# Counting the routed rows on VectorE instead of TensorE, in a two-layer attention and mixture-of-experts kernel

## The reference

```python
# layer 0, experts: 4096 rows, 8 choices (7 experts, 512 places each, and a no-op)
topk_vals, topk_idx = jax.lax.top_k(softmax(x @ router_w.T + router_b), 2)
expert_mask = (rows chosen by each expert)
sorted_indices = jnp.argsort(-expert_mask, axis=0)[:cap]      # the first 512 rows of each expert
h = relu(inputs @ experts_inter); out = (h @ experts_out) * weight     # added back at the rows' places
# layer 1, experts: 12 choices (8 experts and 4 that return the row), nothing is dropped
topk_logits, topk_idx = jax.lax.top_k(x @ gate_w.T + expert_bias, 2)
out = sum over the two of softmax weight * (expert's silu block, or x itself)
```

## Time and profile before

| | |
|---|---|
| median of 3 runs | 1630.83 us (1629.79 to 1632.42) |
| profiled execution | 1632.42 us, with a span of 1630.9 us |
| busy, PE / PEld / DVE / ACT / POOL | 85% / 59% / 54% / 43% / 30% |
| chain that ended last, by engine | PE 51%, DVE 5%, issue 5%, ACT 4%, DMA 3%, POOL 1% |
| TensorE's granted clock, mean | 0.925 of full speed |
| the five matmuls of `ps` | 16 times, once for each sequence in each layer |

### The profile page before, as it was taken

How to read it: one execution, slowest core, us unless ns; L and a number is a source line. 1 busy time by engine, 2 the same in 40 slices (tenths; PEclk the granted TensorE clock), 3 DMA queues, 4 the chain that set the end, 5 groups by cost and what they waited for, 6 DMA issues and landing times.

```text
span 1630.9 us, 31041 instructions
## 1 busy us (share of the span) xinstructions
PE 1383.5 (85%) x10703; PEld 959.3 (59%) x10704; DVE 879.5 (54%) x2705; ACT 702.2 (43%) x984; POOL 496.1 (30%) x415
## 2 busy tenths in 40 slices
PE   3779998999988289999449999999998659999991
PEld 1456666666655256767225555655655449999991
DVE  1667878778885311111357776776552443444344
ACT  2144555555556111110145767767777212222223
POOL 4032344334425311221111132233212134444442
PEclk7799999999999589999779999999999769999996
DMA  6845446536612035351165645644554434444446
GB/s 166 219 104 121 106 109 147 123 99 150 122 45 88 17 78 146 85 148 14 39 130 104 124 88 123 147 105 94 124 119 136 143 93 66 74 71 71 70 62 218
DMA packets 119545, 174.71 MB, mean 107 GB/s; under 512 B 17623, under 2 KB 101617, under 8 KB 113280
## 3 DMA queue, kind: packets, MB, share of 16 engines
q1 hardware_dynamic: 96320, 148.05, 37.5%
q0 software_dynamic: 20400, 22.37, 8.6%
q10 hardware_dynamic: 2704, 2.70, 0.5%
HBM read 107.64 MB, written 72.69 MB: 111 GB/s over the span
## 4 chain that ended last, share of the span: by engine, by line
PE 51%; DVE 5%; issue 5%; ACT 4%; DMA 3%; POOL 1%; SPq 1%; POOLq 0%; ACTq 0%; DVEq 0%
PE ST L1887 8%; PE shared L1899 7%; PE ST L1345 6%; PE ST L753 6%; PE OT L771 6%; PE shared L1547 3%; ACT arena L897 3%; PE OT L1355 3%; PE shared L1355 3%; PE shared L802 2%; PE shared L819 2%; PE shared L1554 1%; PE shared L783 1%; DMA arena<-qk_parts 1%; PE shared L1877 1%
## 5 line engine op out<-in xcount | busy, mean ns | idle before, releaser
L897 ACT ACTIVATE arena<-ST 128x1024 f32<-128x1024 f32 x416 | 411.6, 1024 | 207.2 <-PE ST L753 206.2
L753 PE MATMUL ST<-arena 96*128 96x256 bf16 (+2 forms) x1792 | 243.1, 270 | 36.6 <-DMA arena<-qk_parts 21.1
L771 PE MATMUL OT<-arena,v_aug 128*32 128x256 f32 (+1 forms) x3584 | 233.4, 375 | 8.2 <-POOL arena L1244 7.9
L753 PEld LDWEIGHTS ST<-arena 96*128 96x128 bf16 (+1 forms) x1792 | 149.9, 99 | 138.2 <-issue 47.8
L1994 POOL DMA_INDIRECT sum<-arena,block_to_row x71 | 112.2, 1581 | 167.9 <-DMA sum<-arena,block_to_row 115.1
L771 PEld LDWEIGHTS OT<-arena,v_aug 128*32 128x32 f32 x3584 | 91.4, 110 | 98.1 <-issue 47.9
L1899 PE MATMUL shared<-arena 128*128 x568 | 134.2, 379 | 0.0
L1244 POOL TENSOR_SCALAR_AFFINE_SELECT arena<-arena 128x512 f32<-128x512 f32 (+1 forms) x96 | 79.2, 831 | 170.3 <-ACT arena L897 170.3
L1716 POOL DMA_INDIRECT slot_x<-x_out,row_to x64 | 63.6, 994 | 163.5 <-DVE keep L1634 146.5
L1899 PEld LDWEIGHTS shared<-arena 128*128 128x128 f32 x568 | 102.6, 191 | 11.0
L1701 POOL TENSOR_TENSOR qk_src<-qk_rest,qk_src 128x512 bf16<-128x512 f32 x32 | 38.5, 1202 | 222.0 <-DVE qk_src L1671 222.0
(11 more groups left out here) (244 smaller groups left out, 2530.2 us busy)
## 6 DMA issues: line engine op xcount, KB each, us to landing
arena<-qk_parts SPq DMA_DIRECT2D x224, 128.0 KB, 6.9
qk_parts<-qk_src SPq DMA_DIRECT2D x32, 384.0 KB, 2.8
arena<-qk_parts SPq DMA_DIRECT2D x32, 384.0 KB, 4.6
qk_parts<-qk_src SPq DMA_DIRECT2D x64, 192.0 KB, 3.2
arena<-slot_x SPq DMA_DIRECT2D x71, 130.0 KB, 2.4
arena<-qk_parts SPq DMA_DIRECT2D x32, 256.0 KB, 5.4
sum<-x_out SPq DMA_DIRECT2D x16, 512.0 KB, 2.9
arena<-in_experts_inter SPq DMA_DIRECT2D x7, 1024.0 KB, 5.0
```

Of the source, the lines that this page charges most:

```text
L753: mm = pe.matmul(scores[:, i * 256 + at:i * 256 + at + nq], K[par][0:rows, h, kb * P:(kb + 1) * P], Q[par][0:rows, h, q0:q0 + nq], start=T ...
L771: mm = pe.matmul(OT[32 * i:32 * i + 32, q0:q0 + nq], v_aug[par][:, kb, g * GH + i, :], PT[n % RING][:, i, at:at + nq], start=(u == 0), sto ...
L897: act.activation(PT[n % RING][:, :, :], scores[:, :].rearrange("p (h n) -> p h n", h=GH), func, scale=ATT_SCALE).then_inc(L["exp"], 1)
```

## The change

The per-block sums move from TensorE to VectorE. A new tile `r_before` (128 by 5 by 12, bf16) replaces `r_carry` and `r_count`. Behind the mask, `count_before` copies block 4 of it to block 0 and then adds the mask block by block: five instructions, each waited for by the next, since each reads what the last one wrote. `ps` becomes eight matmuls of 8 or 12 columns, two for each block. It waits for the end of the five. The reduction and the carry's addition in `l3` go. In the schedule, `l2` has five more pieces in both layers, and stage A has four fewer spaces ahead of `ps`.

```diff
-N_ROUTE = {True: (3, 17, 11), False: (13, 0, 11)}
+N_ROUTE = {True: (3, 22, 11), False: (13, 5, 11)}
-SPACES = {True: (4, 2, 2, 0, 8), False: (4, 2, 4, 2, 4)}
+SPACES = {True: (4, 2, 2, 0, 4), False: (4, 2, 4, 2, 4)}
...
-                sums = bank[:, 0:TB * ne].rearrange("p (t e) -> p t e", t=TB)
-                pe.matmul(sums, before[:, :], r_mask[:, :, 0:ne], start=True, stop=False, skip_group_check=True)
-                for t in range(1, TB):
-                    pe.matmul(sums[:, t:TB, :], ones_b[:, :], r_mask[:, 0:TB - t, 0:ne], start=False, stop=False,
-                              skip_group_check=True)
-                pe.matmul(sums, ones_b[:, :], r_carry[k % 2][:, 0:ne].unsqueeze(1).broadcast_to([P, TB, ne]),
-                          start=False, stop=True, skip_group_check=True).then_inc(ready, 1)
+                for t in range(TB):
+                    pe.matmul(bank[:, t * ne:(t + 1) * ne], before[:, :], r_mask[:, t, 0:ne],
+                              start=True, stop=False)
+                    mm = pe.matmul(bank[:, t * ne:(t + 1) * ne], ones_b[:, :], r_before[:, t, 0:ne],
+                                   start=False, stop=True)
+                mm.then_inc(ready, 1)
...
-        def count_rows(dve, chain, ne):
-            chain.unwaited(dve.tensor_reduce(r_count[:, 0:ne], r_mask[:, :, 0:ne].rearrange("p t e -> p e t"),
-                                             AX_X, ALU.add))
-        def carry_on(dve, chain, ne, k):
-            chain.unwaited(dve.tensor_tensor(r_carry[(k + 1) % 2][:, 0:ne], r_carry[k % 2][:, 0:ne], r_count[:, 0:ne],
-                                             ALU.add))
+        def count_before(dve, chain, ne):
+            yield from chain(dve.tensor_copy(r_before[:, 0, 0:ne], r_before[:, TB, 0:ne]))
+            for t in range(TB):
+                yield from chain(dve.tensor_tensor(r_before[:, t + 1, 0:ne], r_before[:, t, 0:ne], r_mask[:, t, 0:ne],
+                                        ALU.add))
...
                 yield from chain(dve.tensor_tensor(r_mask[:, :, 0:ne], oh[0], oh[1], ALU.add))
+                yield from count_before(dve, chain, ne)
...
-                        act.wait_ge(L["rc"], k * ROUTE1 + MASK1 - 1)
+                        act.wait_ge(L["rc"], k * ROUTE1 + MASK1 - 5)
```

More of the change, by code:

```diff
@@ L542, in build @@
         r_mask = sb("r_mask", [P, TB, NEM], BF16)
-        r_carry = [sb(f"r_carry{i}", [P, NEM], BF16) for i in range(2)]
-        r_count = sb("r_count", [P, NEM])
+        r_before = sb("r_before", [P, TB + 1, NEM], BF16)
         row_to = [sb(f"row_to{i}", [P, TB, 2], I32) for i in range(2)]
@@ L595, in build @@
         TOLD, PLACED = 4, 6
-        ROUTE0 = 20 + 2 + TOLD + 1 + 2 + PLACED
+        ROUTE0 = 25 + TOLD + 1 + 2 + PLACED
         LN_CHAIN = TB + TB + 1 + RSQRT_STEPS
@@ L1099, in a_route_dve @@
                 wait(dve, L["scattered"][par], half * (16 * 2 * TB))
-                count_rows(dve, chain, ne)
                 tell_slot(dve, chain, par, k, r_s[:, 4, :], r_s[:, 5, :])
@@ L1108, in a_route_dve @@
                 banks.read(dve, turn, ("ps", 0))
-                carry_on(dve, chain, ne, k)
                 yield from chain(dve.tensor_tensor(r_s[:, 12:14, :], r_oh[:, :, :, E0], r_s[:, 4:6, :], ALU.mult))
@@ L1129, in a_dve @@
             dve.memset(ones_b[:, :], 1.0).then_inc(s_fill, 1)
-            dve.memset(r_carry[0][:, :], 0.0).then_inc(s_fill, 1)
+            dve.memset(r_before[:, :, :], 0.0).then_inc(s_fill, 1)
             for i in range(2):
@@ L1258, in a_pool @@
             slots(pool, emit)
-        MASK0 = 3 + 3 + 5 + 1 + 5 + 3
+        MASK0 = 3 + 3 + 5 + 1 + 5 + 3 + 5
         LANE_RANK0, LANE_CAP, LANE_SEG0, LANE_RB0 = 0, 16, 32, 48
@@ L1436, in build @@
         COMB = NORM + TB + 3 + RSQRT_STEPS + 1 + TB + 1
-        MASK1 = 5 + 1 + 5 + 2
-        ROUTE1 = MASK1 + 2 + TOLD + PLACED + 3
+        MASK1 = 5 + 1 + 5 + 2 + 5
+        ROUTE1 = MASK1 + TOLD + PLACED + 3
         ROPE = 5
@@ L1613, in c_route_dve @@
                 yield from chain(dve.tensor_tensor(r_mask[:, :, 0:ne], oh[0], oh[1], ALU.add))
+            elif step == "l2":
+                chain = Chain(dve, L["rc"], k * ROUTE1)
+                chain.n = MASK1 - 5
+                yield from count_before(dve, chain, ne)
                 assert chain.n == MASK1, chain.n
@@ L1646, in c_dve @@
                     dve.tensor_scalar(cols, cols, rn_scale[:, side, c:c + 1], None, ALU.mult).then_inc(s_w1s, 1)
-            dve.memset(r_carry[0][:, :], 0.0).then_inc(s_fill2, 1)
+            dve.memset(r_before[:, TB, :], 0.0).then_inc(s_fill2, 1)
             dve.wait_ge(s_fill2, 3)
@@ L1865, in d_pe @@
             pe.wait_ge(LC["oe"], NB * NG)
-            pe.matmul(shared[0][:, 0:E1], ones_b[:, :], r_carry[NB % 2][:, 0:E1], start=True, stop=True
+            pe.matmul(shared[0][:, 0:E1], ones_b[:, :], r_before[:, TB, 0:E1], start=True, stop=True
                       ).then_inc(d_cnt, 1)
```

## The result

The changed kernel took 1652.28 us (median; 1651.45 to 1654.45) where the kernel before took 1631.62 beside it (1629.79 to 1633.96): ratio 1.0134, 95% interval 1.0120 to 1.0148. It is slower, as forecast, but by 20.7 us and not by 5.1, and the time lies above the forecast's upper end of 1641.

The account below looks back on a forecast made before the run. PE (85% busy) was taken as the bound, VectorE's small instructions costing only where waited for. Terms 1.0 + 1.0 + 3.5 + 0.3 - 0.6 + 0.4 + 0 - 0.5 = +5.1 gave 1635.9 us against the median; whole range 1630.5 to 1641.

Parts of the forecast that it names:

- The five instructions: Copy and four additions behind each mask on VectorE: each 0.17 long, 0.20 apart, 1.0 us for five where waited for.
- Ninth turns, +1.0 each: Last turns of A and C: the five lie between mask and `ps`, net +1.0 us each, range 0.3 to 1.2.
- `ps` +0.08: TensorE's `ps`: eight matmuls in place of five take 0.08 us more.
- Body turns of A, +0.7: A's five body turns: new `ps` wait replaces the select's; VectorE's longer queue delays `o_nat` 0.7 us each, +3.5 in all.
- The clock: the rival: A's body turns: longer wait for `o_nat` drops TensorE's clock, +3.6 us or more, giving 1639.5; chance 0.10.
- Hidden in A: Rival: A's body turns hide the five, so the 3.5 us goes, giving 1632.4; chance 0.20.
- only the number counts: Rival: only VectorE's instruction count matters, 0.6 us in place of 1.0 or 0.7, giving 1634.6; chance 0.05.
- Clock kept in the eighth turns: Rival: earlier logits in A's and C's eighth turns keep TensorE's clock up, -6.1 us, giving 1629.8; chance 0.07.
- Seventh and eighth turns of A: Seventh: VectorE's 0.7 less 0.4 for earlier logits, +0.3 us; eighth: transpose and copy moved ahead, -0.6 us.
- C's body, +0.08: C's five body turns: another chain's waits hide the five; PE pays 0.08 us each for longer `ps`, +0.4 in all.
- C's seventh turn, 0: Mask chain adds 1.0 + 0.08 us, earlier logits give back 1.1; net 0, from -0.6 to 1.1.
- C's eighth turn, -0.5: Two blocks of scores and one `av` go behind the logits, whose wait was 2.64; -0.5 us, from -2.6 to 0.5.

Follow-up runs that it names:

- e10: The changed kernel with the four additions in A's body turns moved ahead of the maximum, right behind the copy; ratio 1.0095 to the kernel before.
- e18: The changed kernel with `qk_rest` back ahead of the maxima in A's body turns, copy and additions right behind it; ratio 1.0030 to the kernel before.
- e9: The kernel before with only the schedule's numbers set as in the changed kernel, the count made as before; ratio 1.0069 to the kernel before.
- e11: As e10, but with four reductions not waited for one by one in place of the four additions; ratio 1.0061 to the kernel before.
- e17: As e9, but with the subtraction `qk_rest` put back ahead of the third-last maxima in A's body turns; ratio 0.9952 to the kernel before.
- e12: The change in stage C alone, stage A as in the kernel before; ratio 1.0021 to the kernel before.
- e5: The kernel before, unchanged, run once more for its trace; ratio 0.9988 to the kernel before.
- e1: The changed kernel with four chained reductions in place of the four additions; ratio 1.0047 to the kernel before, on a chip where that takes 1658.24 us.
- e2: The changed kernel with eight useless matmuls ahead of PE's wait for the count in A's body turns; ratio 1.0078 to the kernel before.
- e16: The changed kernel, run once more for comparison; ratio 1.0110 to the kernel before.

## Why the prediction was right and wrong

**The five instructions: right.** 0.17 long and 0.20 apart, 0.76 for the four additions in both ninth turns, and in A's body too where nothing holds them (e10, e18).

**Ninth turns, +1.0 each: right.** PE's waits grew by 0.99 and 1.00, the time from mask to `ps` by 1.00 twice. **`ps` +0.08: right**, by C's body turns of 55.84 and 55.92, and by the time from its first matmul to `av` behind it (0.21 before, 0.27 after).

**Body turns of A, +0.7: wrong, and this is the step that failed.** Four of them grew by 9.36, 2.34 each. The forecast had two parts. In the first, the last addition was put at the mask's start + 1.70 (0.60 for the maximum, 4 x 0.20), so a wait of 0.77 at `ps`; it came at + 2.59 with a wait of 1.74. The text noted that the subtraction would go behind the select, and took from it only that PE's wait for the select would go. It did go. But the select, earlier by 1.5 us against the mask, now stood beside VectorE's additions, and an addition that reads two tiles in SBUF was held until the select's end. The addition of 0.2 had been priced from a place in which GpSimd was idle. The trace of before had the sign, in VectorE's timeline of the same body turn:

```profile
433.37 0.56 DVE L1028 TENSOR_SCALAR x_out<-lane 128x4 f32<-128x4 f32 x1
```

The same instruction is 0.16 long in the earlier trace rows. Here it ends at 433.93, and the select of the earlier trace rows at 433.91.

The second part was VectorE's queue, +0.7. Here the size of the five themselves was right and two holds were missing. From mask to `o_nat` VectorE took 1.86 more (8.88 for 7.02), close to what the clean turn grew by (59.95 for 58.17). By the starts of the rows it is 0.94 for the held addition, 0.25 for the TENSOR_SCALAR (its follower starts 0.72 behind it, before 0.47), and 0.67 for the five less the two that went. In e18, which has the forecast's wait at `ps` (0.81 for 0.77), the wait for `o_nat` is 1.27, up by 0.4, and the clean turn is up by only 0.2. The five are no cheaper there: they take 0.79, net of the two that went. But the TENSOR_SCALAR of 434.35 is now behind the select's end and is no longer held, which gives back 0.41 that the kernel before had lost, and `qk_rest` starts 0.12 sooner.

The order was the other half of the step. It was taken as free in A's body turns, and alone it made them 60.4 (e9), by the same kind of hold.

**The clock: the rival had the right kind of cause, with the wrong place and too small a chance.** It was given 0.10, for a longer wait at `o_nat`: a fall in each of five turns and a second in some, +3.6 or more. The longer wait came at `ps`; the one at `o_nat`, forecast as 1.6, shrank to 0.36. There were nine falls for four, so 15.4 us of full speed lost for 6.8. Part of that is hidden. The turns of after are 1.4 above their clean length and those of before 0.85 above theirs (59.02 on the mean for 58.17), so of the 9.36 the clock has 0.56 a turn, 2.2 in all, and VectorE's path has the other 7.1. The reason for discounting the rival was that the sum of PE's waits would hardly change. It did not: 0.91 + 0.81 + 0.86 = 2.58 against 1.74 + 0.82 + 0.36 = 2.92. What changed was that more of it stood in one piece.

**Hidden in A** and **only the number counts** fell. e10 and e11 have the same number, and 0.76 against 0.50 for the four. The rule of the Trainium skill ("VectorE: DVE Perf Modes", section "The DRAIN you can't avoid") does not hold for instructions that wait for one another here. **Clock kept in the eighth turns** fell too: A's lost 3.4 us to the clock in both kernels, C's 6.3 in after and 5.2 in before.

**Seventh and eighth turns of A: too low, and the wrong sign.** +0.3 and -0.6 were forecast for steps that moved; they came to +1.35 and +1.82. In the order alone (e17, of another chip) they were 51.0 and 39.7 against 51.5 and 40.1 in the trace of before, so the steps themselves did gain a little; the five in the way, one of them held, and one fall more in the seventh took it back. **C's body, +0.08: too low**, +0.43, by +0.35 of the new order, which had been taken as free. **C's seventh turn, 0: near**, +0.23. **C's eighth turn, -0.5**: -2.4 by the order (e17) and +0.44 with the five. In that turn e17 lost 3.4 to the clock, before 5.2, e12 and e18 6.8. Why the five bring two falls back there stays open.

Of the rest, B has +1.40, and there the clock took 2.8 us more than in before (39.3 for 36.6); D and E have -2.80, and there it took 3.1 less (27.6 for 30.7). None of these stages was changed, apart from the tile that D's count reads, and the kernel before itself differs by as much from run to run: in e5 its spans went from 1629.6 to 1636.9. Why the clock differs there is not known.

## What to carry to other kernels

When a change moves a step, look at what the other engines do at the new place, above all at GpSimd beside VectorE: price the instruction from a row that has the same neighbour. The place of one subtraction and of the additions beside it was worth 13 of the 18 us. Count PE's waits by their longest piece, not by their sum: in A's body turns a wait of 1.7 to 3.0 was followed by a fall in nearly every turn, and three of up to 1.3 mostly were not. Ask also what would hide the fall. And when one wait is removed, look at which is next behind it (from `ps` to `o_nat` in e1, e2 and e10) before counting a gain.

## What was not expected of the hardware

VectorE and GpSimd exclude each other for some instructions. Held in VectorE were additions of 128x8 bf16 (1.10 instead of 0.16) and a subtraction of 128x512 f32 (1.49 instead of 0.69) beside the select, each until about its end, and TENSOR_SCALAR and COPY of 128x4 and 128x8 (0.81 beside GpSimd's subtraction, 0.54 beside a select at 493.02). Reductions were not (e1). The other way round GpSimd is held: its select of 136.34 in after, begun behind a `qk_rest` of 136.03, lasts 1.34 instead of 1.10. The Trainium skill says so ("SBUF — State Buffer", section "Who interferes with whom"): a VectorE instruction with two inputs in SBUF waits for a GpSimd instruction that reads SBUF, whichever starts first has the ports to its end, and a reduction never contends. This case's traces agree in each of these points, and the rule would have given the held addition's 0.94 beforehand. The held TENSOR_SCALAR and COPY have one input each, so this rule of two inputs is not what held them.

The clock fell in places that shift from run to run: the same kernel before had four falls in A's body turns in one execution and one in another. One fall lasted 3.4 us each time (two of them in a row 6.8), which is 1.7 of full speed; what it cost the turn went from nothing (59.93 in e16, with a fall behind `ps`) to most of that (60.55 in e10, behind `o_nat`, though VectorE's path is 0.8 shorter there). And the same kernel took 1633 to 1635 on three chips and 1658 and 1664 on two; why was not tried.
